# Two low one-hots of an edge unit from one VectorE comparison instead of two

## The reference

```
# layer 0: relation matrices as mixtures of 8 bases
msg  = sum_b (x[src] @ weight[b]) * w_comp[etype][:, b] * norm
x    = layernorm(x + relu(segment_sum(msg, dst) + bias))
# layer 1
neigh = segment_sum(x[src] + edge_attr, dst)
h     = ((1 + eps) * x + neigh) @ W1 + b1
h     = relu(batchnorm(h))
x     = layernorm(x + h @ W2 + b2)
```

## Time and profile before

| what | value |
|---|---|
| median of three runs | 607.67 us (607.59 to 607.95) |
| span of the profiled execution | 747.0 us |
| DVE busy | 459.0 us, 61% of the span |
| PE busy | 559.9 us, 75% |
| POOL busy | 402.4 us, 54% |
| ACT busy | 218.1 us, 29% |
| line 1608, the low one-hots | 416 instructions, 106.9 us |
| line 1611, the key one-hots | 416 instructions, 131.9 us (67.9 and 64.0) |
| granted TensorE clock, mean | 0.860 |

### The profile page before, as it was taken

How to read it: one execution, slowest core, us unless ns; L and a number is a source line. 1 busy time by engine, 2 the same in 40 slices (tenths; PEclk the granted TensorE clock), 3 DMA queues, 4 the chain that set the end, 5 groups by cost and what they waited for, 6 DMA issues and landing times.

```text
span 747.0 us, 12780 instructions
## 1 busy us (share of the span) xinstructions
PE 559.9 (75%) x3965; PEld 467.9 (63%) x3965; DVE 459.0 (61%) x1813; ACT 218.1 (29%) x323; POOL 402.4 (54%) x434
## 2 busy tenths in 40 slices
PE   5477565569466786777897787877798887798996
PEld 3247565557456665566666675656677776697866
DVE  6587656466666475876556966666754253365466
ACT  9602323233323232333232322232321000000257
POOL 6556666656666656575655655655656566400000
PEclk9999777669687798796887799988899898999998
DMA  5312434355335455464544755574646365554102
GB/s 118 98 44 71 145 125 151 124 158 163 123 124 176 140 177 170 149 192 140 172 156 106 244 154 179 162 239 137 227 128 213 95 204 165 168 168 140 57 3 86
DMA packets 98728, 108.18 MB, mean 145 GB/s; under 512 B 10965, under 2 KB 85702, under 8 KB 98658
## 3 DMA queue, kind: packets, MB, share of 16 engines
q1 hardware_dynamic: 79666, 77.81, 31.6%
q0 software_dynamic: 13312, 27.29, 13.0%
q10 hardware_dynamic: 5680, 2.23, 1.2%
HBM read 81.73 MB, written 25.56 MB: 144 GB/s over the span
## 4 chain that ended last, share of the span: by engine, by line
PE 56%; issue 18%; DVE 15%; another core or an unknown queue 6%; ACT 2%; DVEq 1%; DMA 1%; SPq 0%; ACTq 0%
PE psum L1219 14%; PE psum L1136 12%; PE psum L1127 10%; PE psum L1160 9%; PE psum L1194 5%; DVE etype_hot L1611 2%; DVE etype_hot L1608 2%; DVE adj_flat L1468 2%; DVE sums_flat L1739 2%; PE psum L1362 1%; PE psum L1155 1%; DVE weighted L1496 1%; PE psum L1385 1%; DVE sums_flat L1688 1%
## 5 line engine op out<-in xcount | busy, mean ns | idle before, releaser
L828 POOL DMA_INDIRECT gathered_flat<-in_x_dram,src_i x416 | 400.2, 962 | 245.4 <-issue 97.1
L913 ACT ACTIVATE adj_flat<-psum 128x500 f16<-128x500 f32 (+1 forms) x208 | 127.4, 612 | 359.4 <-remote 197.4
L1127 PE MATMUL psum<-hot,attrs 128*128 128x60 f32 (+3 forms) x832 | 171.9, 294 | 20.4 <-issue 17.0
L1127 PEld LDWEIGHTS psum<-hot,attrs 128*128 128x128 f32 x832 | 160.9, 227 | 34.3 <-issue 31.1
L1136 PE MATMUL psum<-weighted,gathered_flat 128*128 128x96 f32 (+1 forms) x832 | 155.8, 314 | 16.4 <-issue 16.4
L1608 DVE TENSOR_SCALAR etype_hot<-iota_key,gathered_flat 128x128 f16<-128x128 f16 x416 | 106.9, 257 | 93.1 <-remote 57.7
L1136 PEld LDWEIGHTS psum<-weighted,gathered_flat 128*128 128x128 f32 x832 | 138.6, 228 | 17.1 <-issue 17.1
L1160 PE MATMUL psum<-etype_hot 128*128 128x300 f16 (+1 forms) x416 | 138.7, 361 | 11.4 <-issue 6.5
L1611 DVE TENSOR_SCALAR etype_hot<-iota_key,key_t 128x300 f16<-128x300 f16 (+1 forms) x416 | 131.2, 317 | 0.0
L1155 PE MATMUL psum<-twin_hot,etype_hot 128*128 128x25 f16 x182 | 36.5, 200 | 84.9 <-issue 79.5
L1739 DVE TENSOR_TENSOR sums_flat<-psum,sums_flat 128x180 f32 x208 | 71.2, 342 | 36.5 <-remote 12.9
(11 more groups left out here) (158 smaller groups left out, 376.2 us busy)
## 6 DMA issues: line engine op xcount, KB each, us to landing
attrs<-in_edge_attr_dram SPq DMA_DIRECT2D x51, 512.0 KB
adjacency<-adj_flat SPq DMA_DIRECT2D x26, 900.0 KB
gathered_flat<-in_x_dram,src_i POOLq DMA_INDIRECT x416
coef<-adjacency SPq DMA_DIRECT2D x23, 288.0 KB
sums_flat<-adjacency SPq DMA_DIRECT2D x9, 576.0 KB
sums_flat<-adjacency SPq DMA_DIRECT2D x13, 288.0 KB
sums_flat<-adjacency SPq DMA_DIRECT2D x6, 432.0 KB
sums_flat<-adjacency SPq DMA_DIRECT2D x3, 360.0 KB, 3.8
```

Of the source, the lines that this page charges most:

```text
L828: pool.indirect_dma_start(gathered[:, t % (RING * GROUP), :], None, x[:, :], bass.IndirectOffsetOnAxis(src_i[:, t:t + 1], 0)).then_inc(gat ...
L913: nc.scalar.activation(window, counts, ACT.Copy).then_inc(counts_copied, 1)
L1127: product = nc.tensor.matmul(echoed_row(u, i), attrs[:, s * GROUP + j, :], hot_tiles(s, i)[:, u % GU, :].unsqueeze(1) .to_broadcast([P, EC ...
```

## The change

`low_t` becomes a table of 16-bit floats: the same slice of `gathered_flat`, of half the width, read as F16. The numbers 0 to 127 are exact in it. The two `tensor_scalar` instructions of a unit that compare 128 elements with a scalar column become one `tensor_tensor` of 256 elements, ahead of the two key comparisons. Its first operand is the row 0 to 127, read twice; its second operand is the two columns of `low_t`, each element read 128 times in a row.

```
-        low_t = gathered_flat[:, LOW:LOW + T]
+        low_t = gathered_flat[:, LOW:LOW + T // 2].bitcast(F16)
...
+                lows = low_t[:, u * UNIT:(u + 1) * UNIT]
+                nc.vector.tensor_tensor(low_hot[:, u % KEYRING, :, :],
+                                        iota_key[:, 0:P].unsqueeze(1).to_broadcast([P, UNIT, P]),
+                                        lows.unsqueeze(2).to_broadcast([P, UNIT, P]), ALU.is_equal)
                 for i in range(UNIT):
                     t = u * UNIT + i
-                    nc.vector.tensor_scalar(low_hot[:, u % KEYRING, i, :], iota_key[:, 0:P], low_t[:, t:t + 1],
-                                            None, ALU.is_equal)
                     n = HIGHS * WIDTHS[i]
                     last = nc.vector.tensor_scalar(key_hot[:, u % KEYRING, i, 0:n], iota_key[:, 0:n],
                                                    key_t[:, t:t + 1], None, ALU.is_equal)
```

## The result

The change made the kernel slower. Its median is 615.28 us (614.51 to 616.51, 4 runs), and the kernel before, run beside it on the same chip, took 607.63 us (607.24 to 607.95, 4 runs). The ratio is 1.0121, with a 95% interval of 1.0105 to 1.0138: 7.65 us more. The forecast was 607.9 us with a range up to 612.5 us, so the result lies outside. What happened is the first rival, the held gathers, and it cost more than the 4.0 to 6.1 us that it was given.

What follows compares the result with a forecast made beforehand. No engine was taken to fill the span; the chain of waits ran mostly over PE's products, gathers not the bound. DVE's +2.1 us, 12% on the path, gave 607.67 + 0.25 = 607.9 us, no measurable change; range 604.0 to 612.5 us.

Steps and rivals of the forecast that it cites:

- the first rival: POOL's gathers (line 828) held up by the new two-operand comparison: 4.0 to 6.1 us more, 611.7 to 613.8 us; chance 0.27.
- The price of the instruction: New comparison on DVE, line 1607: 415 to 425 ns busy, 0.336 us to the next start.
- The row of the twins: Line 1602 on DVE, same form with 100 elements: 255 ns busy, 0.17 us to the next start; basis for the price.
- DVE's account: DVE over 208 units: 0.336 us replaces 0.326 us each, +2.1 us; busy time falls some 20 us without the time following.
- The +2.1 us on DVE: Added DVE time, +0.010 us a unit over 208 units; 12% of it on the path, +0.25 us.
- The second rival: New comparison on DVE handles two elements at once, 0.20 us to the next start: 604.5 us, at most 598 us; chance 0.10.
- The third: Rival: low one-hots on DVE no longer held up by POOL, DVE gains 1.6 us, 606.1 us at best; chance 0.08.
- the part on the bound: Opening reading of the profile: no engine fills the span, waits run mostly over PE's products, POOL's gathers run ahead.

Runs made afterwards that it cites:

- e9: The kernel before plus, in each unit, a VectorE maximum over 64 elements with one SBUF operand; 608.41 us, ratio 1.0010.
- e6: The kernel before with the twins' two-operand comparison (line 1602) cut into four comparisons with a scalar column; 609.01 us, ratio 1.0025.
- e8: The changed kernel with its new comparison replaced by an equally long maximum over 256 elements, low one-hots filled once before the loop; 607.09 us, ratio 0.9987.
- e10: The changed kernel again, unaltered, profiled a second time; 615.60 us, ratio 1.0131 to the kernel before.
- e1: The kernel before, unchanged, profiled again with a span of 606.1 us; 607.99 us, ratio 1.0000.
- e2: The changed kernel with its new comparison replaced by a fill of the same 256 elements, low one-hots left out; 608.19 us, ratio 1.0010.

## Why the prediction was wrong

- **The price of the instruction was right.** Line 1607 was forecast at 415 to 425 ns and 0.336 us to the next start; it took 417 ns and 0.335 us. The row of the twins extended at 1.04 ns an element gave this. The rule of the Trainium skill cited there ("Vector Engine (DVE) Microarchitecture Reference", section 5.1), that an element read 16 times over as a source of a two-source instruction ran at one element a cycle, agrees with it.
- **DVE's account was right, and its time counted for little.** The line's busy time fell from 108.6 to 86.8 us without the time following. The +2.1 us on DVE were held to be worth 12%, 0.25 us. In e9 27 us were worth 0.45 us, under 2% (5% at the top of its interval), and in e6 20 us went with 1.5 us; none of this makes 2.1 us cost 7.65 us.
- **The second rival** (two elements at once) is refuted by 0.335 us. **The third** (DVE held up less) gave nothing to be seen.
- **The step that failed** is the last of the part on the bound: "POOL waits for PE or for something unnamed for 63.6 and 67.1 us, so in this execution the gathers run ahead and are not the bound". So the sum had no term for POOL. The sentence was true of the execution of 747.0 us alone: in all the later ones, of the kernel before and of every variant, the gathers run back to back. Why that first execution was slower, no run shows. The prediction saw the contradiction itself, in the first rival: the gathers, back to back, and the 98 us after them made 624 us, more than a run takes. That said that POOL can have no idle time to spare in a run, and hence that the gathers are the bound. It was used as an argument for a rival with a chance of 0.27, where it should have replaced the waits of the earlier trace rows. With the gathers as the bound, what the new comparison adds to them is added to the time: 7.4 us more in the row of gathers, and 7.65 us more in the median.
- **The size of the rival was low** as well. The term was "208 x 3/51 = 12 hits of 0.33 to 0.5 us". Measured are 37 held gathers of 0.25 us on average, 9.4 us, and 52 with 11.4 us in all against 18 with 2.9 us before. The rate of 3 in 51 counted hits of the late kind alone, twins that began 0.12 to 0.16 us after the gather. Most hits here are comparisons already under way at the gather's start, or starting with it; a twin of 255 ns is over too soon to cost much that way, and a comparison of 417 ns is not. The top of the range, 612.5 us, had been drawn inside the rival's own 613.8 us.
- The rule of the Trainium skill ("SBUF — State Buffer", the list under its port diagram: a VectorE instruction with two SBUF inputs takes part in the lock on the ports shared with GpSimd) agrees with e8 and e10, 606.0 and 612.8 us of span, and with line 1741, whose second input lies in PSUM. The section "Who interferes with whom" of that page says that `tensor_reduce` never contends on trn2, and that agrees with the gather at 115.87.

## What to carry to other kernels

Before a wait is read as slack, hold the span of the profiled execution against the times of the runs; where it is far longer, add up the back-to-back time of each engine's longest row of like instructions with what lies before and after it, and take as the bound the one that fills the run. Where GpSimd gathers back to back, a VectorE instruction with two SBUF operands has a second price beside its own time: each one that overlaps a gather's start can hold it almost until it ends. Two forms cost the gathers nothing here, a reduction with one SBUF operand and an addition with one operand in PSUM. A comparison with a scalar column held them less, and a fill held them too, so having few inputs is no safeguard by itself.

## What the runs showed that was not expected

- The hold has a plain form: from the gather's start to the end of the VectorE instruction, less 0.126 us, for 47 of the 49 comparisons of line 1607 that started between 0.25 us before and 0.01 us after the gather. With a start 0.02 to 0.11 us after, none of line 1607 held a gather by more than 0.05 us.
- The same form fits the key comparisons, which have one SBUF operand and a scalar column. In e1, 34 of the 41 that write 375 elements and started in that window held the gather so, by 0.04 to 0.17 us, 2.3 us together. They are a good part of the 6.5 us that the kernel before holds its gathers. Unlike line 1607 they mostly lose when they start with the gather: of nine (both sizes) that started between 0.04 us before and 0.01 us after one, only one held it. So the second SBUF operand is not the only thing that holds a gather; it is the one that the change added. One of the 34, on POOL and on DVE:

```profile
299.83 1.07 POOL L828 DMA_INDIRECT gathered_flat<-in_x_dram,src_i  x1 [0.30 <-issue]
```

```profile
299.77 0.32 DVE L1611 TENSOR_SCALAR etype_hot<-iota_key,key_t 128x375 f16<-128x375 f16 x1
```

- A fill holds gathers too, though it reads nothing from SBUF. In e8 the one fill of the ring before the loop made the longest gather of all, on POOL and on DVE:

```profile
44.69 1.96 POOL L828 DMA_INDIRECT gathered_flat<-in_x_dram,src_i  x1 [0.30 <-issue]
```

```profile
44.39 1.34 DVE L1697 MEMSET etype_hot<- 128x1536 f16 x1 [0.49 <-DVE one_eps L1866]
```

  It ends 1.04 us after the gather's start, and the gather is 1.02 us too long. The page of the Trainium skill named above ("SBUF — State Buffer", "Who interferes with whom") says that an instruction with at most one SBUF input leaves GpSimd alone unless it runs in a two-port mode. By that rule the fill would run in such a mode, which no run here shows. In e2 the fills of 272 ns held 20 gathers by over 0.1 us, 3.3 us in all.
- A fill is also cheaper than a comparison of as many elements: 256 elements moved the next start by 0.19 us, against 0.335 us.
- One comparison cut in two holds nearly as much as the whole: 12.4 against 13.5 and 14.1 us, since the second half follows before the gather gets through.
